# A fused Mamba and attention kernel on one core: convolution taps of half the channels as matrix products, and the first B spread by TensorE

## The chip, the cores and the metric

The kernel runs on one core of a Trainium2 chip. The metric is the device time of one execution in microseconds; smaller is better. In the text, PE is TensorE (PEld its weight loads), DVE is VectorE, ACT is ScalarE, POOL is GpSimd and SP is the engine that issues the transfers. PX, PY, PZ, ring and sums are tensors in PSUM, everything else is in SBUF.

## What is computed

Eight sequences of 256 rows by 256 columns go through a Mamba block and then through a linear attention block, in float32. The core of the first, per batch:

```python
xz = einsum('bsd,ed->bse', xn, in_proj_w)        # xn: normalized, scaled and shifted x
x_in, z = split(xz, 2)                           # 512 channels each
u = silu(causal_conv(x_in, conv_w) + conv_b)     # per channel, 4 taps along the sequence
dt_r, B, C = split(u @ x_proj_w.T, [64, 80])     # B and C: 16 states each
dt = softplus(dt_r @ dt_proj_w.T + dt_proj_b)
h = h * exp(dt * A) + (dt * u) * B               # scan over 256 steps, 512 channels x 16 states
y = sum over states of h * C + u * D_param
x = x + gate * ((y * silu(z)) @ out_proj_w.T)
```

The second block (`q`, `k`, `v`, softmax over q's heads and over k's rows, `k^T v`, `q (k^T v)`, normalization, silu, output product) follows on the same x.

## The kernel before

Channels lie on the 128 partitions, in four blocks (DC = 4); the 256 steps lie along the free axis. The scan of a batch is cut into 16 units: channel block dc, and four of the 16 states (q), so a unit is 128 x 1024. 8 batches make 128 units, numbered g; the text also counts them 0 to 15 in their batch. A unit goes through five steps:

- POOL makes the inputs `dtu * B` into one of ten buffers of `hs` (L530).
- ACT makes the decays `exp(dt * A)`, four instructions into one of the two halves of `ring` (L722).
- DVE scans (L950), and multiplies with C (L957). Of every batch, units 1, 5, 9 and 13 have this product on POOL (L539).
- PE turns and adds the states of the unit into `sums` (L1298, with the skip term L1293 at the start of a channel block).
- After the last unit of a channel block, DVE gates the sum with silu(z) (L964). `gate_y` of block 0 stands behind the products of unit 4 and waits until the sum of unit 3 is made.

Everything else is woven into this by hand. Each engine has a loop over g in which a table of pairs (slot, step) says in which unit a step is issued: step of batch b in g = 16 b + slot. An engine does its entries strictly in the order of the program; ACT can be at most two units ahead of DVE, since `ring` has two halves. Negative slots belong to the batch before: slot -16 is unit 0 of the scans of batch b - 1, so the projections of batch b are made during the first half of these scans. The steps that matter here, in the order in which they depend on each other:

- `in_proj(b, h)` on PE: h = 0 and 1 are the two halves of x_in (two channel blocks each, L1242: four products of 256 columns), h = 2 and 3 are z (L1247). For b >= 2 all four write PX one after the other, so each waits until the one before has been read. Slots -18, -16, -14, -13.
- `conv_last_tap(b, h)` on ACT (L615): the tap without a shift and the bias, from PX into `conv`. Slots -15 and -14.
- `conv_taps(b, h)` on DVE (L916): three shifted taps for two channel blocks, six instructions that read PX and add into `conv`. Slots -16 and -14.
- `copy_z` on ACT (slot -11, L624) empties PX for `in_proj(b, 3)`; the silus of z and of u follow in unit 7, with a table load on either side.
- On PE, `transpose_back` (unit 1), `out_proj` (unit 3, issued before the unit's sum, L1350) and `transpose_y` (unit 3, L1178, waits for ACT's `normalize2` of unit 6) belong to earlier batches.

Batch 0 has a start of its own: x_proj (L1265), the copy of its result `xdbl` (ACT, L654), which SP stores to DRAM and reads back as copies of B and C over all partitions (`broadcast_b`, `broadcast_c`), dt_proj (L1276), softplus, and DVE's own first input (L928), which waits for the first copy of B. `keep_on` is filler work on PE.

## Time and profile before

| | us |
|---|---|
| runs | 569.86, 568.53, 568.95 |
| median | 568.95 |
| profiled execution | 569.01 |
| its span | 567.2 |

| engine | busy, share of the span | instructions |
|---|---|---|
| DVE | 514.6 us, 91% | 566 |
| POOL | 453.0 us, 80% | 318 |
| PE | 437.9 us, 77% | 2456 |
| ACT | 408.6 us, 72% | 897 |

The span is cut by the profile into waits and busy time of each engine. A busy share is an average over the start (34 us), eight batches of scans (some 500 us) and the end (35 us). In a row of the trace in order of time stand the start and the length in us, the engine, the line, the instruction, output and inputs, and how many instructions the row holds; a product of float32 appears as two records, so four products are a row of x8. The ends of PE's records are modelled and overlap the next row's start by some 0.16 us.

### The profile page before, as it was taken

What the parts mean: (1) busy time and instruction counts of PE and PEld (TensorE: products, weight loads), DVE (VectorE), ACT (ScalarE), POOL (GpSimd) and SP (SyncE); (2) the same over time, 40 slices, a digit from 0 to 9 for tenths busy, and PEclk for the clock granted to TensorE, in tenths of its full rate; (3) what the DMA queues carried; (4) which work ended last, traced back from release to release, by engine and by line L of the source; (5) the groups of instructions that cost most, each with busy time, mean ns of one, the idle gap of its engine ahead of it and who ended that gap; (6) DMA issues with size and microseconds to landing.
All of it is one profiled execution on the core that took longest, in us unless ns stands there. A gap on an engine that the chain in (4) does not pass through costs nothing. (4 is left out here: it accounts for less than half of the span.)

```text
span 567.2 us, 7391 instructions
## 1 busy us (share of the span) xinstructions
PE 437.9 (77%) x2456; PEld 361.2 (64%) x2456; DVE 514.6 (91%) x566; ACT 408.6 (72%) x897; POOL 453.0 (80%) x318
## 2 busy tenths in 40 slices
PE   8967666769789787768688678768787777866887
PEld 7646445657676676656576667647674666755776
DVE  2479899999999999999999999999999999999753
ACT  2693677668865998578966999488966988486533
POOL 4049969989998889979998889978997989985121
PEclk8988777896789798998989898998899898779899
DMA  9294032201430044001440045011440045000001
GB/s 269 66 326 125 3 114 85 102 4 54 159 112 0 29 151 154 14 19 40 159 131 1 28 151 165 2 29 43 147 129 1 10 151 166 2 0 20 0 1 37
DMA packets 22366, 45.38 MB, mean 80 GB/s; under 512 B 3685, under 2 KB 13557, under 8 KB 22329
## 3 DMA queue, kind: packets, MB, share of 16 engines
q1 hardware_dynamic: 22328, 44.92, 24.3%
q8 instruction: 19, 0.31, 0.2%
q14 instruction: 19, 0.15, 0.1%
HBM read 42.52 MB, written 2.39 MB: 79 GB/s over the span
## 5 line engine op out<-in xcount | busy, mean ns | idle before, releaser
L530 POOL TENSOR_TENSOR hs<-dtu,Br 128x1024 f32<-128x1024 f32 x127 | 297.0, 2362 | 8.5 <-DMA Br<-bc_rows 8.5
L722 ACT ACTIVATE ring<-dt,Aneg 128x256 f32<-128x256 f32 x512 | 212.9, 465 | 72.6 <-DVE hs L957 68.7
L950 DVE TENSOR_TENSOR_SCAN ring<-ring,hs 128x1024 f32<-128x1024 f32 x97 | 221.4, 2282 | 5.8 <-ACT ring L722 5.4
L1298 PE MATMUL sums<-ident,hs 128*128 128x128 f32 x1024 | 150.7, 303 | 36.3 <-DVE hs L957 36.0
L1298 PEld LDWEIGHTS sums<-ident,hs 128*128 128x128 f32 x1024 | 134.4, 158 | 48.3 <-DVE hs L957 44.7
L957 DVE TENSOR_TENSOR hs<-ring,Cr 128x1024 f32<-128x1024 f32 x97 | 118.8, 1225 | 3.3
L539 POOL TENSOR_TENSOR hs<-hs,Cr 128x1024 f32<-128x1024 f32 x31 | 73.2, 2360 | 42.1 <-DVE hs L950 42.1
L950 DVE TENSOR_TENSOR_SCAN hs<-ring,hs 128x1024 f32<-128x1024 f32 x31 | 70.3, 2269 | 0.0
L1366 PE MATMUL PY<-wqkvo,xT 128*128 128x256 f32 x168 | 46.6, 428 | 0.0
L1293 PE MATMUL sums<-ident,uD 128*128 128x128 f32 x64 | 15.5, 333 | 35.2 <-DVE ygT L964 35.2
L1366 PEld LDWEIGHTS PY<-wqkvo,xT 128*128 128x128 f32 x168 | 37.5, 223 | 6.6
L615 ACT ACTIVATE conv<-PX,par 128x256 f32<-128x256 f32 x28 | 14.3, 560 | 35.8 <-PE PX L1242 35.6
L916 DVE SCALAR_TENSOR_TENSOR conv<-PX,par,conv 128x255 f32<-128x255 f32 (+2 forms) x84 | 33.9, 472 | 6.0 <-ACT conv L615 5.8
L1293 PEld LDWEIGHTS sums<-ident,uD 128*128 128x128 f32 x64 | 9.1, 168 | 38.2 <-DVE hs L957 37.7
L1242 PE MATMUL PX<-xnT,win 128*128 128x256 f32 x112 | 30.6, 421 | 3.6 <-ACT xnT L606 2.5
L1247 PE MATMUL PX<-win,xnT 128*128 128x512 f32 x52 | 27.1, 646 | 4.2 <-DVE conv L916 2.8
L1242 PEld LDWEIGHTS PX<-xnT,win 128*128 128x128 f32 x112 | 22.3, 209 | 8.0 <-ACT xnT L606 3.9
L1350 PE MATMUL PY<-wo,yg 128*128 128x256 f32 x112 | 25.3, 379 | 0.0
L1350 PEld LDWEIGHTS PY<-wo,yg 128*128 128x128 f32 x112 | 21.2, 190 | 5.4 <-issue 2.9
L481 POOL TENSOR_SCALAR ve<-mv 128x2 f32<-128x2 f32 x22 | 4.9, 222 | 24.2 <-DVE mv L899 22.9
L1178 PE MATMUL PZ<-ident,xh 128*128 128x128 f32 x56 | 10.1, 310 | 16.5 <-ACT xh L591 16.5
L1178 PEld LDWEIGHTS PZ<-ident,xh 128*128 128x128 f32 x56 | 7.5, 159 | 21.9 <-ACT xh L591 20.9
(218 smaller groups left out, 694.1 us busy)
## 6 DMA issues: line engine op xcount, KB each, us to landing
Br<-bc_rows SPq DMA_DIRECT2D x32, 512.0 KB, 5.1
Cr<-bc_rows SPq DMA_DIRECT2D x32, 512.0 KB, 4.2
xg<-in_x SPq DMA_DIRECT2D x8, 256.0 KB, 2.9
out<-fin SPq DMA_DIRECT2D x7, 256.0 KB, 4.2
hs<-in_ada_wT SPq DMA_DIRECT2D x3, 512.0 KB, 4.6
win<-in_in_wT SPq DMA_DIRECT2D x2, 512.0 KB, 6.1
hs<-in_W_emb SPq DMA_DIRECT2D x2, 512.0 KB
gate<-gate_rows SPq DMA_DIRECT2D x8, 128.0 KB, 3.1
```

What stands on the lines that cost most here:

```text
L530: nc.gpsimd.tensor_tensor(hs[:, g % DBUF], dtu[:, b % 2, dc, :].unsqueeze(1).to_broadcast([P, NQ, T]), Br[:, NQ * q:NQ * q + NQ, :], ALU.m ...
L539: nc.gpsimd.tensor_tensor(hs[:, g % DBUF], hs[:, g % DBUF], Cr[:, NQ * q:NQ * q + NQ, :], ALU.mult).then_inc(s_hc_pool, 1)
L722: ins = nc.scalar.activation(ring[:, g % 2, j, :], dt[:, b % 2, dc, :], ACT.Exp, scale=Aneg[:, c:c + 1])
L916: V.scalar_tensor_tensor(conv[:, dc, s:], xz_bank(b, h)[:, e, 0:T - s], w, conv[:, dc, s:], ALU.mult, ALU.add).then_inc(s_tap_done, 1)
L950: V.tensor_tensor_scan(driven if by_pool(g) else decays, decays, driven, 0.0, ALU.mult, ALU.add).then_inc(s_scan_done, 1)
L957: V.tensor_tensor(hs[:, g % DBUF], ring[:, g % 2], Cr[:, NQ * q:NQ * q + NQ, :], ALU.mult).then_inc(s_hc_dve, 1)
L1242: ins = M(xz_bank(b, h)[:, e, :], win[:, k, lo:lo + P], xnT[:, k, :], start=(k == 0), stop=(k == KD - 1))
L1247: ins = M(flat(xz_bank(b, h)), xnT[:, k, P * c:P * c + P], win[:, k, DI:2 * DI], start=(k == 0), stop=(k == KD - 1))
L1293: ins = M(YT[:, c, :], uD[:, dc % 2, P * c:P * c + P], ident[:, :], is_transpose=True, start=(c == 0), stop=False, skip_group_check=True)
L1298: ins = M(YT[:, c, :], hs[:, g % DBUF, j, P * c:P * c + P], ident[:, :], is_transpose=True, start=False, stop=(q == UPC - 1 and j == NQ - ...
L1350: ins = M(dst, yg[:, k, P * c:P * c + P], wo[:, k, :], start=(k == 0), stop=(k == DC - 1))
L1366: ins = M(dst, xT_of(b)[:, k, P * c:P * c + P], wqkvo[:, w, k, :], start=False, stop=(k == KD - 1), skip_group_check=True)
```

## The change

There are two parts.

**The taps.** For batches 2 to 7 and h = 1 (`folded`), DVE's six instructions are gone. PE makes the convolution itself: the weights of this half are scaled by each of the four taps, and the four products with xn shifted by 0 to 3 steps are added in PX (`taps_of_block`), per channel block 2 x 4 products instead of 2. The first channel block stands in slot -16, the second in -15. ACT's `conv_last_tap` of that half only adds the bias, and moves from slot -14 to -12. `in_proj(b, 2)` and `in_proj(b, 3)` move one slot back, to -13 and -12, for b >= 2; for batch 1 they stay. The scaled weights are made once by POOL: three of them in the start (`wtap`), from taps that two new transfers of SP spread over the partitions, and the last in unit 14 over the weights themselves.

**The start.** B for unit 0 is spread over the partitions by PE (`first_b`, four products of a column of ones at B's row with `xdbl`, into ring's second half), so DVE's first input reads PSUM instead of waiting for the transfer; the transfer of this part of B goes last but one. DVE copies the first xdbl instead of ACT. ACT does the silu of u's first half ahead of z's, and loads the silu table before it waits. `keep_on` is shorter in two places.

On PE, from the sum of unit 0 to the first row of unit 4 in a batch with folding, before. `sums<-ident,hs` x8 is the sum of a unit (x16 of two), `PX<-xnT,win` the second half of x_in, `PX<-win,xnT` z, `PY<-wo,yg` out_proj, `PZ<-ident,xh` transpose_y:

```order
L1298 MATMUL sums<-ident,hs 128x128 x8
L1242 MATMUL PX<-xnT,win 128x256 x4
L1316 MATMUL PZ<-ident,ygT 128x128 x4
L1316 MATMUL PY<-ident,ygT 128x128 x4
L1298 MATMUL sums<-ident,hs 128x128 x16
L1247 MATMUL PX<-win,xnT 128x512 x2
L1350 MATMUL PY<-wo,yg 128x256 x8
L1298 MATMUL sums<-ident,hs 128x128 x8
L1247 MATMUL PX<-win,xnT 128x512 x2
L1178 MATMUL PZ<-ident,xh 128x128 x4
L1293 MATMUL sums<-ident,uD 128x128 x2
```

The same place after (the first channel block's products are in it, the second's, the same four rows, come behind the transposes and are cut off in the first fence; the second fence goes on from there):

```order
L1382 MATMUL sums<-ident,hs 128x128 x8
L1322 MATMUL PX<-xnT,win 128x256 x2
L1322 MATMUL PX<-xnT,wtap 128x255 x2
L1322 MATMUL PX<-xnT,wtap 128x254 x2
L1322 MATMUL PX<-xnT,wtap 128x253 x2
L1400 MATMUL PZ<-ident,ygT 128x128 x4
L1400 MATMUL PY<-ident,ygT 128x128 x4
L1322 MATMUL PX<-xnT,win 128x256 x2
```

```order
L1382 MATMUL sums<-ident,hs 128x128 x16
L1434 MATMUL PY<-wo,yg 128x256 x8
L1382 MATMUL sums<-ident,hs 128x128 x8
L1306 MATMUL PX<-win,xnT 128x512 x2
L1231 MATMUL PZ<-ident,xh 128x128 x4
L1377 MATMUL sums<-ident,uD 128x128 x2
L1382 MATMUL sums<-ident,hs 128x128 x8
L1306 MATMUL PX<-win,xnT 128x512 x2
```

Sixteen products stand where four stood, ahead of the sums of units 1 to 3; the first half of z is behind the sum of unit 3, and the second half of z behind transpose_y and the sum of unit 4.

On ACT, from the skip term of unit 2 to the copy of z, before (`ring<-dt,Aneg` x4 are the decays of a unit, `conv<-PX,par` is conv_last_tap, `yg` the copies for out_proj, `zs` the copy of z):

```order
L701 ACTIVATE uD<-u,par 128x256
L615 ACTIVATE conv<-PX,par 128x256 x2
L722 ACTIVATE ring<-dt,Aneg 128x256 x4
L731 ACTIVATE yg<-PZ 128x512
L731 ACTIVATE yg<-PY 128x512
L722 ACTIVATE ring<-dt,Aneg 128x256 x8
L624 ACTIVATE zs<-PX 128x512
```

and after:

```order
L746 ACTIVATE uD<-u,par 128x256
L769 ACTIVATE ring<-dt,Aneg 128x256 x4
L778 ACTIVATE yg<-PZ 128x512
L778 ACTIVATE yg<-PY 128x512
L769 ACTIVATE ring<-dt,Aneg 128x256 x4
L658 ACTIVATE conv<-PX,par 128x256 x2
L769 ACTIVATE ring<-dt,Aneg 128x256 x4
L667 ACTIVATE zs<-PX 128x512
```

conv_last_tap of the second half moved behind the decays of unit 4; the copy of z stays behind those of unit 5.

The diff, without the declarations of semaphores:

```diff
--- before.py
+++ after.py
+FOLDED = (1,)
+FOLD_LO, FOLD_N = 2 * P * FOLDED[0], 2 * P * len(FOLDED)
...
+def folded(b, h):
...
+    return b >= 2 and h in FOLDED
...
+def taps_until(b, h):
...
+    return sum(3 * 2 for c in range(b + 1) for k in range(2) if not folded(c, k) and (c, k) <= (b, h))
...
+        wtap = sb("wtap", [P, TAPS - 1, KD, FOLD_N])
...
+        wrow = hs[:, 1, 1:NQ, :]
+        last_row = fin[:, 0, :]
...
-                    broadcast_b(b, 0)
...
+                    broadcast_b(b, 0)
...
+            sp.dma_start(wrow, a["tap_rows"][1:TAPS, FOLD_LO:FOLD_LO + FOLD_N].unsqueeze(0).to_broadcast([P, TAPS - 1, FOLD_N])).then_inc(
+                s_ld_taps, 16)
+            sp.dma_start(last_row, a["tap_rows"][0, FOLD_LO:FOLD_LO + FOLD_N].unsqueeze(0).to_broadcast([P, FOLD_N])).then_inc(
+                s_ld_taps, 16)
...
-                if dc == 0:
+                if dc == 0 or g == UPC:
...
+            def scale_taps():
...
+                pool.wait_ge(s_ld_taps, 32)
+                pool.wait_ge(s_ld_win, 16)
+                for s in range(1, TAPS):
+                    nc.gpsimd.tensor_tensor(wtap[:, s - 1], win[:, :, FOLD_LO:FOLD_LO + FOLD_N],
+                                            wrow[:, s - 1, :].unsqueeze(1).to_broadcast([P, KD, FOLD_N]), ALU.mult).then_inc(s_taps_ready, 1)
+                pool.wait_ge(s_taps_ready, TAPS - 1)
...
+            def scale_last_tap():
...
+                pool.wait_ge(s_xz_mm, 4 + 2)
+                part = win[:, :, FOLD_LO:FOLD_LO + FOLD_N]
+                nc.gpsimd.tensor_tensor(part, part, last_row.unsqueeze(1).to_broadcast([P, KD, FOLD_N]),
+                                        ALU.mult).then_inc(s_taps_ready, 1)
...
+                if g == -6:
+                    scale_taps()
+                if g == 14:
+                    scale_last_tap()
...
+                    tap = 1.0 if folded(b, h) else pcol("conv_w", TAPS * dc + 3, TAPS * dc + 4)
...
-                                         scale=pcol("conv_w", TAPS * dc + 3, TAPS * dc + 4)).then_inc(s_conv0_ready, 1)
+                                         scale=tap).then_inc(s_conv0_ready, 1)
...
             def silu_u(b):
-                act.wait_ge(s_tap_done, 3 * DC * (b + 1))
+                act.wait_ge(s_conv0_ready, DC * (b + 1))
+                act.wait_ge(s_tap_done, taps_until(b, 1))
...
             def copy_xdbl(b):
+                if b == 0:
+                    return
...
-                if b >= 1:
-                    act.wait_ge(s_bc_stored, 16 * b)
+                act.wait_ge(s_bc_stored, 16 * b)
...
+                if g == 1:
+                    act.wait_ge(s_dbu_first, 1)
...
             def silus(b):
...
+                if b == 0:
+                    nc.scalar.preload_act_table_set("silu_and_others")
+                    silu_u_half(0)
...
-                if b == 0:
-                    silu_u_half(0)
-                if b < NB:
...
-                for slot, step in ((-17, normalize0), (-16, modulated), (-15, conv_last_tap_0), (-14, conv_last_tap_1),
+                for slot, step in ((-17, normalize0), (-16, modulated), (-15, conv_last_tap_0), (-12, conv_last_tap_1),
...
-                    late = 2 if step in (conv_last_tap_0, conv_last_tap_1) else 1 if step is modulated else 0
+                    late = 2 if step is conv_last_tap_0 else 1 if step is modulated else 0
...
             def conv_taps(b, h):
...
+                if folded(b, h):
+                    return
...
-                            dve.wait_ge(s_tap_done, 3 * DC * b + 6 * h + 2 * (s - 2) + e + 1)
+                            dve.wait_ge(s_tap_done, taps_until(b, h) - 6 + 2 * (s - 2) + e + 1)
...
+            def first_xdbl():
+                dve.wait_ge(s_xp_mm, 1)
+                V.tensor_copy(xdbl[0:ONES_ROW, :], PX[0:ONES_ROW, 0, :]).then_inc(s_xdbl_ready, 1)
...
-                dve.wait_ge(b_loaded[0], 16)
-                V.tensor_tensor(hs[:, 0], dtu[:, 0, 0, :].unsqueeze(1).to_broadcast([P, NQ, T]), Br[:, 0:NQ, :],
+                dve.wait_ge(s_first_b, 1)
+                V.tensor_tensor(hs[:, 0], dtu[:, 0, 0, :].unsqueeze(1).to_broadcast([P, NQ, T]), ring[:, 1],
...
+                    first_xdbl()
...
+            def wait_x_read(b, h):
...
+                pe.wait_ge(s_conv0_ready, DC * b + 2 * h + 2)
+                if not folded(b, h):
+                    pe.wait_ge(s_tap_done, taps_until(b, h))
...
-                        pe.wait_ge(s_tap_done, 3 * DC * b + 6 * (h - 1))
+                        wait_x_read(b, h - 2)
...
-                    pe.wait_ge(s_tap_done, 3 * DC * b + 6 * h)
+                    wait_x_read(b, h - 1)
...
-                    keep_on(12)
+                    keep_on(4)
...
+            def taps_of_block(b, h, e):
...
+                if e == 0:
+                    wait_x_read(b, h - 1)
+                    if b == 2:
+                        pe.wait_ge(s_taps_ready, TAPS)
+                lo = P * (2 * h + e)
+                for s in range(TAPS):
+                    for k in range(KD):
+                        w = wtap[:, s - 1, k, lo - FOLD_LO:lo - FOLD_LO + P] if s else win[:, k, lo:lo + P]
+                        ins = M(PX[:, e, s:T], w, xnT[:, k, 0:T - s], start=(s == 0 and k == 0),
+                                stop=(s == TAPS - 1 and k == KD - 1), skip_group_check=True)
+                if e == 1:
+                    ins.then_inc(s_xz_mm, 1)
...
+            def first_b():
...
+                pe.wait_ge(s_ld_ident, 16)
+                for n in range(NQ):
+                    row = ident[0:ONES_ROW + 1, RANK + n:RANK + n + 1]
+                    ins = M(ring[:, 1, n, :], row.to_broadcast([ONES_ROW + 1, P]), xdbl[:, :], start=True, stop=True)
+                ins.then_inc(s_first_b, 1)
...
+                if (b, h) == (0, 0):
+                    first_b()
...
-                    keep_on(8)
+                    keep_on(4)
...
             def in_proj_1(b):
-                in_proj(b, 1)
+                if folded(b, 1):
+                    taps_of_block(b, 1, 0)
+                else:
+                    in_proj(b, 1)
...
+            def in_proj_1b(b):
+                if folded(b, 1):
+                    taps_of_block(b, 1, 1)
...
-                for slot, step in ((17, transpose_back), (-19, transpose_x), (-18, in_proj_0), (-16, in_proj_1), (-14, in_proj_2),
-                                   (-13, in_proj_3), (39, output), (-9, x_proj), (-8, dt_proj_0), (-6, dt_proj_1),
+                for slot, step in ((17, transpose_back), (-19, transpose_x), (-18, in_proj_0), (-16, in_proj_1),
+                                   (-15, in_proj_1b), (-13, in_proj_2), (-12, in_proj_3), (39, output), (-9, x_proj), (-8, dt_proj_0), (-6, dt_proj_1),
...
-                    b = due_by(g, slot, -2 if step is in_proj_1 else 2 if step in (in_proj_2, in_proj_3) else 0)
+                    b = due_by(g, slot, -2 if step is in_proj_1 else 1 if step in (in_proj_2, in_proj_3) else 0)
...
+        "tap_rows": np.asarray(L0_cond_conv_w).reshape(DI, TAPS).T[::-1],
...
```

## Rows read from the trace of the kernel before

**Rows 1.** The page: engines' busy time, and two of its groups of instructions.
```profile
PE 437.9 (77%) x2456; PEld 361.2 (64%) x2456; DVE 514.6 (91%) x566; ACT 408.6 (72%) x897; POOL 453.0 (80%) x318
...
L539 POOL TENSOR_TENSOR hs<-hs,Cr 128x1024 f32<-128x1024 f32 x31 | 73.2, 2360 | 42.1 <-DVE hs L950 42.1
...
L916 DVE SCALAR_TENSOR_TENSOR conv<-PX,par,conv 128x255 f32<-128x255 f32 (+2 forms) x84 | 33.9, 472 | 6.0 <-ACT conv L615 5.8
```

**Rows 2.** DVE in order of time, 287 to 323 us: start us, us, engine, line, instruction.
```profile
298.88 1.22 DVE L957 TENSOR_TENSOR hs<-ring,Cr 128x1024 f32<-128x1024 f32 x1
300.25 2.43 DVE L916 SCALAR_TENSOR_TENSOR conv<-PX,par,conv 128x255 f32<-128x255 f32 x6
302.59 0.74 DVE L896 BATCH_NORM_STATS2 st<-qe 128x6 f32<-128x256 f32 x2
...
303.54 2.27 DVE L950 TENSOR_TENSOR_SCAN ring<-ring,hs 128x1024 f32<-128x1024 f32 x1
...
310.44 0.41 DVE L964 TENSOR_TENSOR ygT<-sums,zs 128x256 f32<-128x256 f32 x1
...
313.55 2.29 DVE L950 TENSOR_TENSOR_SCAN ring<-ring,hs 128x1024 f32<-128x1024 f32 x1
...
322.50 2.30 DVE L950 TENSOR_TENSOR_SCAN ring<-ring,hs 128x1024 f32<-128x1024 f32 x1
```

**Rows 3.** PE in order of time, same stretch; in brackets the idle time before.
```profile
293.81 2.08 PE L1428 MATMUL PY<-att,qT 128*128 128x128 f32 x8 [1.13 <-DVE att L1002]
...
297.26 1.89 PE L1242 MATMUL PX<-xnT,win 128*128 128x256 f32 x8
298.99 0.60 PE L1316 MATMUL PZ<-ident,ygT 128*128 128x128 f32 x4
...
302.73 1.98 PE L1247 MATMUL PX<-win,xnT 128*128 128x512 f32 x4 [0.61 <-DVE conv L916]
304.55 3.62 PE L1350 MATMUL PY<-wo,yg 128*128 128x256 f32 x16
308.01 1.04 PE L1298 MATMUL sums<-ident,hs 128*128 128x128 f32 x8
309.34 1.98 PE L1247 MATMUL PX<-win,xnT 128*128 128x512 f32 x4 [0.29 <-ACT zs L624]
313.70 1.11 PE L1178 MATMUL PZ<-ident,xh 128*128 128x128 f32 x4 [2.38 <-ACT xh L591]
...
315.02 1.91 PE L1298 MATMUL sums<-ident,hs 128*128 128x128 f32 x8
```

**Rows 4.** ACT in order of time, same stretch.
```profile
299.19 1.02 ACT L615 ACTIVATE conv<-PX,par 128x256 f32<-128x256 f32 x2 [6.48 <-PE PX L1242]
...
308.71 0.57 ACT L624 ACTIVATE zs<-PX 128x512 f32<-128x512 f32 x1
310.56 1.67 ACT L722 ACTIVATE ring<-dt,Aneg 128x256 f32<-128x256 f32 x4 [1.28 <-DVE hs L957]
...
317.05 0.58 ACT L636 ACTIVATE zs<-PX 128x512 f32<-128x512 f32 x1
...
320.80 2.47 ACT L722 ACTIVATE ring<-dt,Aneg 128x256 f32<-128x256 f32 x6
```

**Rows 5.** Busy time of PE, PEld, DVE, ACT, POOL; granted clock, DMA share, GB/s.
```profile
314.00:318.00 4.00, 3.78 (x22) 3.38 (x21) 3.93 (x7) 3.97 (x8) 4.00 (x3) 0.61 0.01 5
```

**Rows 6.** DVE in order of time, 96 to 133 us: the gating of unit 4, batch 1.
```profile
120.11 0.41 DVE L964 TENSOR_TENSOR ygT<-sums,zs 128x256 f32<-128x256 f32 x1
```

**Rows 7.** DVE, then ACT and POOL, in order of time, in the start.
```profile
32.62 1.23 DVE L928 TENSOR_TENSOR hs<-dtu,Br 128x1024 f32<-128x1024 f32 x1 [1.96 <-DMA Br<-bc_rows]
...
26.47 0.38 ACT L654 ACTIVATE xdbl<-PX 96x256 f32<-96x256 f32 x1
...
30.70 1.67 ACT L722 ACTIVATE ring<-dt,Aneg 128x256 f32<-128x256 f32 x4
...
26.56 0.23 POOL L487 TENSOR_SCALAR nb<-nb 128x2 f32<-128x2 f32 x1
```

3 lines of the change are left out of this document (added).

## Prediction

> **What bounds the kernel now.** I read the page first, then which engine waits for which, then DVE, PE and ACT in order of time through one batch, and last the start. DVE is busy 91% of the span [rows 1]. In the scan part it has next to no idle time, so whatever makes DVE wait there sets the time. The stretch from 287 to 323 us holds units 0 to 8 of batch 4 of the scans, and the projections of batch 5 are made in it. It repeats alike in scan batches 2 to 6. Who is close behind DVE in it:
>
> - DVE's taps of the second half stand at 300.25, behind the products of unit 2; the next entry starts 2.34 us later, at 302.59 [rows 2].
> - PE starts the attention product at 293.81, released by DVE, and works almost without a gap until 311: the idle times printed are 0.61 and 0.29 us [rows 3]. Of what DVE needs, it is little ahead: the sum of unit 3 takes from 308.01 to 309.05 [rows 3], and DVE's gating L964, which needs it, starts at 310.44 [rows 2].
> - ACT waits 6.48 us before the second half's convolution, and once more 1.28 before 310.56 [rows 4]. From 310.56 it has no gap: decays of unit 6, skip term, normalize, decays of unit 7, two table loads around the silus, then the decays of unit 8 from 320.80. Four decays take 1.67 [rows 4], so these end at 322.47, and DVE's scan of unit 8 starts at 322.50 [rows 2].
>
> So the 91% hides two other engines, with 1.4 and 0 us of slack, at two points just behind the edit.
>
> **The change, part by part.**
>
> *DVE's taps go.* Six batches lose six instructions each (all of them in before: 96, of 472 ns [rows 1]). By starts a group costs 302.59 - 300.25 = 2.34 us [rows 2], 14.0 in six. If nothing else moved, that is the gain.
>
> *PE's products come, in units 0 and 1.* The old block of four starts at 297.26 and its follower at 298.99: 1.73 us, 0.43 each [rows 3]. Now there are 16, 12 more: 12 x 0.43 = 5.2 us, where PE has no gap. in_proj_2 goes from before out_proj to behind the sum of unit 3: that takes 304.55 - 302.73 = 1.82 out ahead of the sum, and the 0.61 of idle time, a wait for the removed taps [rows 3]. The sum of unit 3 starts at 308.01 + 5.2 - 1.82 - 0.61 = 310.8. It takes 0.9 (1.04 less the 0.16 by which neighbouring rows overlap), so it ends at 311.7.
>
> *DVE meanwhile.* The products of unit 2 end at 298.88 + 1.22 = 300.1; stats2 takes 0.95 (302.59 to 303.54), scan and products of units 3 and 4 some 3.45 each (from 303.54 to 310.44 both) [rows 2]. So DVE reaches the gating at 308.0. ACT keeps up: its wait in unit 2 is gone, and its copies of yg follow transposes that end 1.7 us later. DVE waits from 308.0 to 311.7, and the gating comes 1.3 us *later* than before, the saved 2.34 notwithstanding.
>
> *ACT behind it.* in_proj_2 follows at 311.7 and takes 1.98 [rows 3]: 313.6. ACT's copy of z (0.57) needs it and stands ahead of the decays of unit 6. Before, it was done at 309.28, in idle time [rows 4]. Now these decays start at 314.1 instead of 310.56, 3.5 us later. Having no gap from there, ACT carries these 3.5 to scan 8 whole.
>
> *PE again.* transpose_y, formerly behind in_proj_3, is now ahead of it, and waits for normalize2, which stands behind those decays. Before, it started 313.70 - 310.56 = 3.14 after them [rows 3, 4]; now at 317.2. The transposes and the sum of unit 4 took 3.2, from 313.70 to 316.93 [rows 3]; over 314 to 318 the granted clock was 0.61, mostly the lower of its two levels (1.2 of 2.4 GHz), after PE had stood idle 2.38 us [rows 3, 5]. This time it stands idle from 313.6 to 317.2, so I take the same 3.2: in_proj_3 starts at 320.4, ends at 322.4. ACT wants it for the second silu of z, 317.05 - 310.56 = 6.49 after its decays [rows 4], at 320.6, and waits 1.8. From there to the decays of unit 8 it is 3.75 (317.05 to 320.80), so these start at 326.1 instead of 320.80: **+5.3 us**. With the transposes and the sum at the upper level (1.6) it would be +3.8. I take 5.0, nearer to the slow value since the idle time ahead grows. DVE scans unit 6 at 314.1 + 1.67 = 315.8, reaches unit 8 the old 8.95 later, at 324.7, and waits 3.1 for the decays. Behind unit 8 the distances are the old ones and DVE bounds again, so nothing is given back. Scan batches 2 to 6: 5 x 5.0 = 25.0.
>
> *Scan batch 1* has neither attention nor transpose_y yet, so PE has more room. Its cost lies between 0 and 5.3; its gating of unit 4 stood at 120.11 [rows 6]. The copy of z is late there too, in_proj_3 is not; I take 1.9. Scan batches 0 and 7 have no folded half.
>
> *The start.* Before, DVE's first input waits 1.96 us for the transfer of B, starts at 32.62 and takes 1.23, and the first scan follows at 33.9 [rows 7]. With B from PE this wait goes; next are the decays, from 30.70, which end at 32.37 [rows 7]. u ahead of z brings x_proj forward by up to the 0.6 of one silu. But ACT's normalization, which follows, is held by POOL's nb, done at 26.79, and ACT already started it behind xdbl (26.47 to 26.85) [rows 7]; so this part gives 0.1 to 0.3. The first scan starts at some 32.1: -1.8. What hides the rest: the four products for B (0.43 each, or double at the lower level) lie beside ACT's softplus; on SP the other copies of B and C move one place forward, and B 0, now last, is next wanted for unit 4; POOL's three scalings fall where it has nothing to do yet, each half the size of one of 2360 ns [rows 1], the fourth where it is ahead, and its waits for DVE's scans, 42.1 us in all [rows 1], are the cover. SP's two new transfers (0.5 MB) go out before its long wait for xdbl. Bounds: 0, if the wait for in_proj_2 in unit 5 takes it back, and -3, if all of the 1.96 and the time of u arrive.
>
> **Sum.** The profiled execution took 569.0 (span 567.2 and 1.8 around it), the median of the runs is 568.95, the same. 569.0 + 25.0 + 1.9 - 1.8 = **594.1 us**, 4.4% slower. Own range: 3.8 to 5.8 in five batches, 0 to 5.3 in batch 1, 0 to -3 at the start, not all at one end: 583 to 604.
>
> **A rule weighed.** PE is busy 77% on average and DVE 91% [rows 1], which makes moving work from DVE to PE look free. In the rows of the stretch PE has no gap. The Trainium skill (Perfetto Trace Analysis, Identifying Performance Opportunities) says to optimize the engine with the highest occupancy first, and that PE's busy share is no good measure of its headroom. By the first half of this the time would be the first rival's; by the rows it is the forecast's.
>
> **Rivals.**
>
> 1. *PE has the room, and DVE's saving arrives* (faster): 569.0 - 14.0 - 1.8 = 553 us. It needs PE's products to cost next to nothing beside the old ones: 313.6 for in_proj_2 less 5.2 is 308.4, and DVE is at the gating at 308.0. The point from which it decides: in_proj_2 done by 310.0, that is 12 products in 1.6 us, 0.13 each. For it speaks PE's average; against it 0.43 us by starts for this shape, already at the upper level [rows 3].
> 2. *PE's clock pays for half.* If its higher load holds the upper level, the attention product and the sum behind it are 1.4 us shorter, the transposes and sum 4 1.6 shorter. Then scan 8 is some 2.3 later than before: 569.0 + 5 x 2.3 + 1 - 1.8 = 580. Against it: the lower level follows PE's waits of 1.13 and 2.38 us [rows 3, 5], and these stay or grow. The Trainium skill (TensorE: Matmul & The Clock Gate, Part 1) says that activity releases the throttle, which would speak for it.
> 3. *More is late.* The lower level also catches in_proj_3 (1.98 becomes some 3.7): +7 a batch, 604 and more.
> 4. *It cancels out*: 569. I see no mechanism.
>
> **Chances.** Forecast (583 to 604) 0.72; second rival (567 to 583, most of it above 574) 0.12; third 0.05; first, or a part of it, 0.09; fourth 0.02. The range 574 to 604 holds 0.82. A measurement of this kernel tells about 0.2% from no change. Faster by more than that 0.09, within it 0.02, slower 0.89.
>
> **What would show it.** Right: in scan batches 2 to 6 DVE idle for 3 to 4 us before the gating of unit 4, released by PE's sum, and some 3 us before the scan of unit 8, released by ACT; ACT waiting for PE before the copy of z and before the second silu of z; these batches each some 5 us longer from first scan to first scan, batch 1 some 2; the first scan at 32.1. Wrong: each batch 2 us shorter, with these waits under a microsecond (first rival); or a granted clock near 1 behind the transposes (second); or the decays of unit 8 not behind in_proj_3.

## The result, and the profile after

The changed kernel takes 592.23 us (median of 4, 591.25 to 593.18); the kernel before, in the same session, 569.40 (median of 4, 568.53 to 571.23). The ratio is 1.040, 95% interval 1.037 to 1.042: **slower by 4%**. The profiled execution took 592.05. The forecast was 594, slower.

Its page, engines' busy time, against [rows 1]:

```profile
span 590.3 us, 7643 instructions
...
PE 470.4 (80%) x2592; PEld 390.6 (66%) x2592; DVE 503.2 (85%) x531; ACT 407.2 (69%) x896; POOL 457.7 (78%) x322
```

DVE lost 35 instructions and 11.4 us of work, PE gained 32.5, and the span grew by 23.1. DVE's idle time is where it went. In the view of who waits for whom stand the engine and line, the releaser, the us in total, the times and the longest; before, the first of these two waits was 5.4 us in 6 times, and the second stood only once for 1.2, in the end:

```profile
DVE ring L1002 <- ACT ring L769: 23.7, 15, 4.2
DVE ygT L1016 <- PE sums L1382: 20.0, 8, 3.6
```

By batch, from the start of the scan of one unit 0 to the next (for batch 7, to the scan of its last unit):

| scan batch | 0 | 1 | 2 | 3 | 4 | 5 | 6 | 7 |
|---|---|---|---|---|---|---|---|---|
| before, us | 65.1 | 60.7 | 63.7 | 63.5 | 63.3 | 63.5 | 63.1 | 55.4 |
| after, us | 65.0 | 61.4 | 66.7 | 68.3 | 68.3 | 68.3 | 68.3 | 56.1 |

Batch 4 begins at 293.90, 6.88 later than before (287.02); subtract 6.88 to set the next rows beside [rows 2 to 4]. DVE in order of time (start us, us, engine, line, instruction, in brackets the idle time before it and who ended it):

```profile
313.60 1.22 DVE L1009 TENSOR_TENSOR hs<-ring,Cr 128x1024 f32<-128x1024 f32 x1
318.43 0.42 DVE L1016 TENSOR_TENSOR ygT<-sums,zs 128x256 f32<-128x256 f32 x1 [3.60 <-PE sums L1382]
...
322.33 2.30 DVE L1002 TENSOR_TENSOR_SCAN ring<-ring,hs 128x1024 f32<-128x1024 f32 x1 [0.70 <-ACT ring L769]
...
334.42 2.30 DVE L1002 TENSOR_TENSOR_SCAN ring<-ring,hs 128x1024 f32<-128x1024 f32 x1 [3.21 <-ACT ring L769]
```

PE in the same stretch:

```profile
300.69 2.08 PE L1512 MATMUL PY<-att,qT 128*128 128x128 f32 x8 [0.73 <-DVE att L1054]
...
304.41 1.03 PE L1322 MATMUL PX<-xnT,win 128*128 128x256 f32 x4
305.27 2.73 PE L1322 MATMUL PX<-xnT,wtap 128*128 128x255 f32 x12
307.84 0.60 PE L1400 MATMUL PZ<-ident,ygT 128*128 128x128 f32 x4
...
317.36 1.04 PE L1382 MATMUL sums<-ident,hs 128*128 128x128 f32 x8
318.23 1.88 PE L1306 MATMUL PX<-win,xnT 128*128 128x512 f32 x4
323.77 0.66 PE L1231 MATMUL PZ<-ident,xh 128*128 128x128 f32 x4 [3.66 <-ACT xh L633]
...
324.48 1.81 PE L1382 MATMUL sums<-ident,hs 128*128 128x128 f32 x8
326.08 2.83 PE L1306 MATMUL PX<-win,xnT 128*128 128x512 f32 x4
```

And ACT:

```profile
320.15 0.60 ACT L667 ACTIVATE zs<-PX 128x512 f32<-128x512 f32 x1 [5.40 <-PE PX L1306]
320.64 1.66 ACT L769 ACTIVATE ring<-dt,Aneg 128x256 f32<-128x256 f32 x4
...
328.95 0.60 ACT L679 ACTIVATE zs<-PX 128x512 f32<-128x512 f32 x1 [1.73 <-PE PX L1306]
...
332.72 3.26 ACT L769 ACTIVATE ring<-dt,Aneg 128x256 f32<-128x256 f32 x8
```

Read it as one chain. The 8 products of one column block (16 entries of the trace) take 307.84 - 304.41 = 3.43 us, and there are two blocks: 6.9 us where the old four products took 1.73 [rows 3]. So the sum of unit 3 ends at some 318.2, and DVE stands 3.60 us before the gating. in_proj_2 is next; only when it is done can ACT copy z, and the decays of unit 6 stand behind that copy. Then PE idles 3.66 for ACT's normalization and makes in_proj_3 late, so ACT idles 1.73 for it. The decays of unit 8 start at 332.72, in the old count 325.84 against 320.80: 5.04 us late. DVE waits 3.21 for them. The new waits (3.60, 0.70 and 3.21) less the 2.34 of taps that are gone make 5.2, against 5.04 of longer period.

### The profile page after: what moved, and what is told of

Same layout as the page of the kernel before. It is cut to its first block and busy times, and to the rows that moved or that the text cites. A ratio compares the mean times of both kernels' runs of the same rounds, so it can differ in the third digit from the quotient of the medians.

```text
span 590.3 us, 7643 instructions
## 1 busy us (share of the span) xinstructions
PE 470.4 (80%) x2592; PEld 390.6 (66%) x2592; DVE 503.2 (85%) x531; ACT 407.2 (69%) x896; POOL 457.7 (78%) x322
## 5 line engine op out<-in xcount | busy, mean ns | idle before, releaser
L1382 PE MATMUL sums<-ident,hs 128*128 128x128 f32 x1024 | 148.7, 302 | 17.4 <-DVE hs L1009 17.4
L1450 PE MATMUL PY<-wqkvo,xT 128*128 128x256 f32 x168 | 48.5, 441 | 0.0
L1450 PEld LDWEIGHTS PY<-wqkvo,xT 128*128 128x128 f32 x168 | 39.3, 234 | 7.3
L1322 PE MATMUL PX<-xnT,wtap 128*128 128x255 f32 (+2 forms) x144 | 32.8, 377 | 0.0
L667 ACT ACTIVATE zs<-PX 128x512 f32<-128x512 f32 x7 | 4.2, 597 | 40.0 <-PE PX L1306 40.0
L1016 DVE TENSOR_TENSOR ygT<-sums,zs 128x256 f32<-128x256 f32 x32 | 13.3, 416 | 20.0 <-PE sums L1382 20.0
L1322 PEld LDWEIGHTS PX<-xnT,wtap 128*128 128x128 f32 x144 | 27.4, 190 | 3.5
L1306 PE MATMUL PX<-win,xnT 128*128 128x512 f32 x52 | 29.3, 695 | 0.0
L1231 PEld LDWEIGHTS PZ<-ident,xh 128*128 128x128 f32 x56 | 6.1, 141 | 34.2 <-ACT xh L633 33.9
L964 DVE SCALAR_TENSOR_TENSOR conv<-PX,par,conv 128x255 f32<-128x255 f32 (+2 forms) x48 | 19.4, 472 | 5.7 <-ACT conv L658 5.7
L1434 PEld LDWEIGHTS PY<-wo,yg 128*128 128x128 f32 x112 | 20.7, 190 | 2.5
```

The source lines that it names most:

```text
L964: V.scalar_tensor_tensor(conv[:, dc, s:], xz_bank(b, h)[:, e, 0:T - s], w, conv[:, dc, s:], ALU.mult, ALU.add).then_inc(s_tap_done, 1)
L1306: ins = M(flat(xz_bank(b, h)), xnT[:, k, P * c:P * c + P], win[:, k, DI:2 * DI], start=(k == 0), stop=(k == KD - 1))
L1322: ins = M(PX[:, e, s:T], w, xnT[:, k, 0:T - s], start=(s == 0 and k == 0), stop=(s == TAPS - 1 and k == KD - 1), skip_group_check=True)
L1382: ins = M(YT[:, c, :], hs[:, g % DBUF, j, P * c:P * c + P], ident[:, :], is_transpose=True, start=False, stop=(q == UPC - 1 and j == NQ - ...
L1434: ins = M(dst, yg[:, k, P * c:P * c + P], wo[:, k, :], start=(k == 0), stop=(k == DC - 1))
L1450: ins = M(dst, xT_of(b)[:, k, P * c:P * c + P], wqkvo[:, w, k, :], start=False, stop=(k == KD - 1), skip_group_check=True)
```

## Experiments

Twelve kernels ran. In the table each stands with its own runs of the kernel before.

| run | us, median (n) | before | ratio, 95% interval |
|---|---|---|---|
| e1 start alone | 567.56 (12) | 569.78 | 0.997 (0.996 to 0.999) |
| e2 taps alone | 593.02 (4) | 569.78 | 1.041 (1.039 to 1.044) |
| e3 no shifted products | 571.54 (10) | 569.78 | 1.003 (1.000 to 1.005) |
| e4 before, PE delayed | 594.28 (4) | 569.78 | 1.043 (1.041 to 1.046) |
| e5 in_proj_3 early | 574.53 (5) | 569.61 | 1.008 (1.005 to 1.011) |
| e6 e3 and e5 together | 558.53 (4) | 569.61 | 0.979 (0.975 to 0.983) |
| e7 start alone, bias late | 569.77 (12) | 569.61 | 1.001 (0.998 to 1.003) |
| e8 folded, reordered | 558.98 (5) | 569.61 | 0.981 (0.978 to 0.984) |
| e9 e8, sum 4 first | 556.34 (6) | 569.31 | 0.978 (0.974 to 0.982) |
| e10 e9, bias on GpSimd | 555.16 (6) | 569.31 | 0.975 (0.972 to 0.979) |
| e11 e8 without folding | 571.59 (10) | 569.31 | 1.005 (1.003 to 1.008) |
| e12 e10, scaling later | 554.46 (6) | 569.32 | 0.974 (0.970 to 0.977) |

### The two halves of the change apart: e1 and e2

e1 is the changed kernel with no folded half and without what serves it alone:

```
 def folded(b, h):
-    return b >= 2 and h in FOLDED
+    return False
...
-                if g == -6:
-                    scale_taps()
-                if g == 14:
-                    scale_last_tap()
```

> The start of the change alone (first input from TensorE's copy of B, u ahead of z, fewer filler products); all taps are VectorE's again, and the tap rows and GpSimd's four scaling operations are gone. Theory T (the start gives what it gave in the changed kernel, first scan 1.5 us earlier; and the 2.4 us which VectorE lost at unit 8 of batch 0 came from GpSimd's shifted phase behind the last scaling, so it does not come back here): 565.5 to 568, ratio 0.993 to 0.998, the 128x8 operation of unit 8 in batch 0 again near 0.23 us. Rival S (the time of unit 8 moves with the start itself): first scan 1.5 earlier, unit 8 late again, 568.5 to 569.5.

e2 keeps the folding and undoes the start: SP's old order of copies, ACT's copy of xdbl, the input from `Br`, z ahead of u, the old fillers.

```
-                    act.wait_ge(s_dbu_first, 1)
...
-                dve.wait_ge(s_first_b, 1)
+                dve.wait_ge(b_loaded[0], 16)
...
-                    first_xdbl()
```

> The taps of the change alone; the start is as before. Theory T (12 more products per batch ahead of the sums of units 1 to 3, in_proj_2 behind the sum of unit 3, in_proj_3 behind the transposes of the second normalisation): +4.6 to +5.2 per batch in batches 3 to 6, +3 in batch 2, +1 to +2 in batch 1, +0.8 in batch 7, in all 592 to 595, ratio 1.039 to 1.046. Rival S (a part of the loss comes from the start's changed phase): under 590.

Both times are as theory T had them; of its parts one missed, batch 1 of e2 grew by 0.75 and not by 1 to 2. The start is worth -2.2 us (0.8 to 2.5 by the interval), the taps +23.2, together 21.0; the whole was 22.8, which their intervals don't tell apart. The periods of e2 are those of the changed kernel within 0.05 us in batches 1 to 6. One reason in e1's expectation was wrong: the small operation at unit 8 of batch 0 took 1.48 us, not 0.23. It has a section of its own below.

### What PE's time ahead of the sum costs: e4

```
                     c = h - 2
-                    for k in range(KD):
-                        ins = M(flat(xz_bank(b, h)), xnT[:, k, P * c:P * c + P], win[:, k, DI:2 * DI], start=(k == 0),
-                                stop=(k == KD - 1))
+                    for _ in range(4 if b >= 2 and h == 2 else 1):
+                        for k in range(KD):
+                            ins = M(flat(xz_bank(b, h)), xnT[:, k, P * c:P * c + P], win[:, k, DI:2 * DI], start=(k == 0),
+                                    stop=(k == KD - 1))
```

> The kernel before, VectorE's taps kept, with in_proj_2 of batches 2 to 7 made four times into the same bank (the same result), 6 more products, 5 to 6 us more of TensorE ahead of the sum of unit 3; nothing is taken from any engine. Theory T (TensorE's work ahead of the sum of unit 3 comes out in the gating product's wait): the gating wait in batches 3 to 6 is 2.5 to 5 us, periods +2.5 to +5, in all 583 to 595. Rival R (TensorE at 77% busy has room for 5 us in the stretch): periods +0.5 at most, 569 to 572.

Nothing was taken from DVE or ACT, and the time is that of the changed kernel. PE and DVE of e4 in batch 4:

```profile
314.08 7.13 PE L1248 MATMUL PX<-win,xnT 128*128 128x512 f32 x16 [0.37 <-DVE conv L916]
```
```profile
325.58 0.42 DVE L964 TENSOR_TENSOR ygT<-sums,zs 128x256 f32<-128x256 f32 x1 [3.71 <-PE sums L1299]
```

The equal time is no evidence by itself, since it is made up differently: 4.7 us in batch 1, where the gating waits 4.63, and 3.4 to 4.5 in each of batches 2 to 6. The wait is the evidence. The 6 products more (12 entries) made in_proj_2 7.13 us long instead of 1.98 [rows 3], 5.15 more, and of this 3.71 came out as DVE's wait at the gating; the other 1.4 was the slack of the sum of unit 3 that the prediction had read off (309.05 against 310.44 [rows 2, 3]). With PE at 79% busy there was no room for 5 us in this place. (Unit 8 has no wait in e4 in batches 2 to 5, so e4 shows the first of the changed kernel's two large waits and not the second.) Rival R, the first rival of the prediction in another coat, is out.

### The products, or their order: e3, e5, e6

e3 leaves the 12 shifted products of each folded half out and keeps the order of all engines:

```
-                for s in range(TAPS):
+                for s in range(1):
```

> The changed kernel without the 12 products of the shifted taps of each folded half, from batch 2 on: the shifted taps of channels 256 to 511 are left out of what is computed, their unshifted tap stays (TensorE makes 4 products there, as before), VectorE makes none of them, the order of all engines is that of the changed kernel. Theory T (the length of the products is the cost): the gating product of unit 3 no longer waits for TensorE for over 0.5 us, the period of batches 3 to 6 is 62.0 to 63.8 us, in all 561 to 570. Rival O (the new order of TensorE, with in_proj_2 behind the sum of unit 3 and in_proj_3 behind the transposes, is the cost, whatever the length): periods over 65, in all over 578.

Both theories missed. The gating's wait went to nothing, as T said; but 571.5 is above T's range, and the periods of batches 2 to 4 are 64.2 to 64.6 (63.1 and 63.3 in 5 and 6). DVE has 2.34 us less work in each batch, waits 2.3 to 3.9 at unit 8, where the kernel before waited 0.08, and so gives all of it back. ACT, PE and DVE of e3, batch 4:

```profile
318.73 0.60 ACT L679 ACTIVATE zs<-PX 128x512 f32<-128x512 f32 x1 [2.98 <-PE PX L1306]
```
```profile
312.30 1.11 PE L1231 MATMUL PZ<-ident,xh 128*128 128x128 f32 x4 [3.66 <-ACT xh L633]
...
315.34 3.36 PE L1306 MATMUL PX<-win,xnT 128*128 128x512 f32 x4
```
```profile
324.20 2.30 DVE L1002 TENSOR_TENSOR_SCAN ring<-ring,hs 128x1024 f32<-128x1024 f32 x1 [3.88 <-ACT ring L769]
```

So the place of in_proj_3, behind transposes that wait for ACT, has a price of its own without the long products. Part of it is PE's clock: the granted clock was 0.50 over 312 to 316, and in_proj_3 took 3.36 us where [rows 3] has 1.98. e5 moves it alone, one slot forward, in the complete changed kernel; e6 does so in e3, so it too leaves the shifted taps out:

```
-                                   (-15, in_proj_1b), (-13, in_proj_2), (-12, in_proj_3), (39, output), (-9, x_proj), (-8, dt_proj_0), (-6, dt_proj_1),
+                                   (-15, in_proj_1b), (-13, in_proj_2), (-13, in_proj_3), (39, output), (-9, x_proj), (-8, dt_proj_0), (-6, dt_proj_1),
...
-                    b = due_by(g, slot, -2 if step is in_proj_1 else 1 if step in (in_proj_2, in_proj_3) else 0)
+                    b = due_by(g, slot, -2 if step is in_proj_1 else 1 if step is in_proj_2 else 2 if step is in_proj_3 else 0)
```

> The changed kernel with in_proj_3 straight behind in_proj_2, ahead of the transposes of the second normalisation instead of behind them and the sum of unit 4. Theory T2 (the loss has two parts: the products' length, which comes out at the gating product, and in_proj_3's place, which comes out at scan 8 through the second silu): the wait of that silu (1.73 us) goes, scan 8 waits 1.4 to 1.7 us instead of 3.21, periods of batches 3 to 6 about 66.6, in all 582 to 585. Rival (the place of in_proj_3 is free, since ScalarE's chain is bound elsewhere): within 2 us of 592.

> The changed kernel without the 12 products of the shifted taps of each folded half (they are left out of what is computed; the unshifted tap stays) and with in_proj_3 straight behind in_proj_2: the run without the products, and without the one piece of order that is under suspicion. Theory T2: the run that only left the products out lost at scan 8 what VectorE saved, 3.2 to 3.9 us of wait, of which the silu's wait for TensorE was 2.98; here that wait is gone, scan 8 waits under 1 us, periods 61.0 to 61.8, in all 556 to 561. Rival (something else of the order holds ScalarE): periods stay over 63, 568 or more.

The silu's wait of 1.73 is gone in e5, scan 8 waits 1.36 (expected 1.4 to 1.7). But the time fell by 17.7 us, not by 8: the periods are 64.83 in all of batches 2 to 6, 1.9 less in batch 2 and 3.5 less in the others. Most of the rest is this row of PE, which stands ahead of anything that was moved, and the gating behind it:

```profile
294.12 1.16 PE L1512 MATMUL PY<-att,qT 128*128 128x128 f32 x8 [1.14 <-DVE att L1054]
```
```profile
310.23 0.42 DVE L1016 TENSOR_TENSOR ygT<-sums,zs 128x256 f32<-128x256 f32 x1 [1.96 <-PE sums L1382]
```

The attention product took 1.16 us instead of 2.08, the sum behind it 1.04 instead of 1.59, and the gating waited 1.96 instead of 3.60. That is PE's clock, at its upper level here (granted clock 1.00 over 293 to 297), which is taken up below. So the 17.7 us are 5 x 1.85 at unit 8 (3.21 less 1.36), the order; 4 x 1.64 at the gating of batches 3 to 6, the clock; and some 2 in the start and in batches 1 and 7. e6 gives 558.5, within its range of 556 to 561, with periods of 61.4 and a wait of 0.79 at scan 8. The four corners:

| | 12 products made | left out |
|---|---|---|
| in_proj_3 behind the transposes | 592.2 | 571.5 |
| in_proj_3 straight behind in_proj_2 | 574.5 | 558.5 |

Leaving the products out gives 20.7 in the one order and 16.0 in the other; moving in_proj_3 gives 17.7 and 13.0. The first is the length, the second the order together with the clock. The order without the clock is some 9 of the 17.7, as just added up. The prediction's sum had both in it, the length and the 1.8 us of in_proj_3's place.

### A kernel that keeps the products and is faster: e8 and e11

e8 leaves nothing out. Its moves: out_proj from ahead of the sum of unit 3 to behind it (3.46 us out of the gating's way); in_proj_3 ahead of the sum of unit 4 instead of behind it, still behind the transposes of the second normalization, but with ACT's normalization for them already in unit 4, where ACT idled for 1.23 and 5.40 us; the first z turned into its silu straight from PSUM, without the copy; and the second z's silu last of the silus.

```
-                b = due(g, 19)
-                if b is not None:
-                    out_proj(b)
                 if 0 <= g < NB * U and not by_pool(g):
...
-                for slot, step in ((17, transpose_back), (-19, transpose_x), (-18, in_proj_0), (-16, in_proj_1),
-                                   (-15, in_proj_1b), (-13, in_proj_2), (-12, in_proj_3), (39, output), (-9, x_proj), (-8, dt_proj_0), (-6, dt_proj_1),
+                for slot, step in ((17, transpose_back), (19, out_proj), (-19, transpose_x), (-18, in_proj_0), (-16, in_proj_1),
+                                   (-15, in_proj_1b), (-13, in_proj_2), (35, transpose_y), (-13, in_proj_3), (39, output), (-9, x_proj), (-8, dt_proj_0), (-6, dt_proj_1),
...
-                for slot, step in ((-17, normalize0), (-16, modulated), (-15, conv_last_tap_0), (-12, conv_last_tap_1),
+                for slot, step in ((-17, normalize0), (-16, modulated), (-15, conv_last_tap_0), (36, normalize2), (-12, conv_last_tap_1),
...
             def copy_z(b):
-                if b == 0:
+                if b != 1:
                     return
...
+                elif b >= 2:
+                    act.wait_ge(s_xz_mm, 4 * b + 3)
+                    act.wait_ge(s_ygT_ready, DC * (b - 1))
+                    nc.scalar.activation(zs[:, b % 2, 0, :], flat(xz_bank(b, 2)), ACT.Silu).then_inc(s_z_ready, 2)
...
+                if 1 <= b < NB:
+                    silu_z_second(b)
```

> The changed kernel with five moves, nothing left out: TensorE's out_proj behind the sum of unit 3 instead of ahead of it; then in_proj_2, the transposes of the second normalisation, in_proj_3, then the sum of unit 4; ScalarE's second normalisation in unit 4, ahead of the copy of the folded half, where ScalarE idles; no copy of the first z but its silu straight from PSUM; u's silu and the transposed y's ahead of the second z's. Theory T2: the gating product no longer waits 3.6 us (under 0.9), ScalarE's chain from decays 6 to decays 8 shortens from 12.1 to about 9.6 us, scan 8 waits under 1 us, periods 61.0 to 62.3, in all 556 to 562: TensorE's 12 products fit in once what else stands ahead of the sum is moved. Rival (TensorE has no room for them at any order, it then delays the gating product of unit 7, or the dt chain of the next batch): periods 64 or more, 570 or more.

e11 has the same moves and no folding.

> The five moves of the folded and reordered kernel without the folding: VectorE makes all taps, TensorE 4 products for the second half, the start is the changed one. Theory T2 (the moves only make room for TensorE's products; without them VectorE sets the time): 566 to 570, ratio 0.994 to 1.002, periods of batches 2 to 6 of 63 to 64 us. Rival (the moves are worth something by themselves, and the folding nothing): 562 or less.

e8 is 558.98, 33 us below the changed kernel and 1.9% below the one before. DVE, ACT and PE of e8 in batch 4:

```profile
303.05 0.41 DVE L1020 TENSOR_TENSOR ygT<-sums,zs 128x256 f32<-128x256 f32 x1
...
315.85 2.30 DVE L1006 TENSOR_TENSOR_SCAN ring<-ring,hs 128x1024 f32<-128x1024 f32 x1 [0.72 <-ACT ring L771]
```
```profile
308.77 0.60 ACT L674 ACTIVATE zs<-PX 128x512 f32<-128x512 f32 x1
...
312.23 0.60 ACT L681 ACTIVATE zs<-PX 128x512 f32<-128x512 f32 x1 [1.00 <-PE PX L1310]
```
```profile
309.42 2.77 PE L1310 MATMUL PX<-win,xnT 128*128 128x512 f32 x4 [2.22 <-ACT zs L674]
```

The gating has no wait, scan 8 has 0.72, the periods of batches 3 to 6 are 61.4 (62.9 in batch 2). The moves were made together; what each is worth no run shows. e11 came out at 571.6, 1.6 above its range. DVE in batch 3 of e11, and the out_proj that it waits for:

```profile
249.41 0.69 DVE L1020 TENSOR_TENSOR x<-PY,gate 128x512 f32<-128x512 f32 x1 [1.50 <-PE PY L1430]
```
```profile
243.74 5.64 PE L1430 MATMUL PY<-wo,yg 128*128 128x256 f32 x16
```

out_proj stands late, and at the lower clock (5.64 us instead of 3.62) it is too late for `gate_x`, which waits for it in four batches, 4.4 us in all. So the moves cost some 4 us over e1, and are worth nothing by themselves. In the new order folding is worth 571.6 - 559.0 = 12.6 us, but 4 of these are e11's own loss. Against e1, the better of the two kernels without folding, e8 gains 8.6 us, and the changed kernel loses 24.7 (592.2 less 567.6). The same twelve products.

### The idle time ahead of in_proj_3: e9

```
-                                   (-15, in_proj_1b), (-13, in_proj_2), (35, transpose_y), (-13, in_proj_3), (39, output), (-9, x_proj), (-8, dt_proj_0), (-6, dt_proj_1),
+                                   (-15, in_proj_1b), (-13, in_proj_2), (35, transpose_y), (-12, in_proj_3), (39, output), (-9, x_proj), (-8, dt_proj_0), (-6, dt_proj_1),
...
-                    b = due_by(g, slot, -2 if step is in_proj_1 else 1 if step is in_proj_2 else 2 if step is in_proj_3 else 0)
+                    b = due_by(g, slot, -2 if step is in_proj_1 else 1 if step in (in_proj_2, in_proj_3) else 0)
```

> The folded and reordered kernel with one move: in_proj_3 behind the sum of unit 4 instead of ahead of it, so that TensorE does not stand idle for 2.2 us ahead of in_proj_3. In the folded and reordered run in_proj_3 took 2.8 us at the lower clock, the second z's silu waited 1.0 us for it, and scan 8 0.72. Theory K (the lower clock behind TensorE's idle time is what that wait is made of): in_proj_3 takes 1.9 us, the silu waits under 0.3 us, scan 8 under 0.1, 0.6 to 0.7 less in each of batches 3 to 6, in all 555.5 to 556.5. Rival (the clock stays low, since TensorE still idles for about a microsecond there): 558.5 to 559.5.

In batches 2, 3 and 5 the theory holds: in_proj_3 takes 1.98 (2.77 in e8, behind 2.2 us of idle time; here PE is idle 1.1), in batch 5 the silu waits 0.22, DVE has no wait, and the period is 60.6, nearly all of it DVE's work. Batch 6 is as long, with a wait of 0.88 at unit 8. The time is 556.34 (553.5 to 559.3), as expected within its spread. Batch 4 is 62.9 long: DVE waits 1.04 for decays, 0.26 at the gating and 0.83 for out_proj. PE in it, and in batch 5:

```profile
285.16 2.08 PE L1516 MATMUL PY<-att,qT 128*128 128x128 f32 x8 [1.13 <-DVE att L1058]
```
```profile
348.10 1.16 PE L1516 MATMUL PY<-att,qT 128*128 128x128 f32 x8 [1.13 <-DVE att L1058]
```

### The small operations beside GpSimd: e7, e10, e12

At unit 8 of batch 0, DVE makes four 128x8 operations. Before, they took 0.23 us each, beside an idle GpSimd. DVE and POOL of the changed kernel:

```profile
72.26 0.41 DVE L1120 TENSOR_SCALAR m1s<-mods,par 128x8 f32<-128x8 f32 x1
72.59 2.40 DVE L1120 TENSOR_SCALAR m1b<-mods,par 128x8 f32<-128x8 f32 x1
74.90 0.22 DVE L1120 TENSOR_SCALAR m1s<-mods,par 128x8 f32<-128x8 f32 x1
```
```profile
71.38 1.27 POOL L591 TENSOR_TENSOR win<-win,fin 128x512 f32<-128x512 f32 x1
72.60 2.36 POOL L552 TENSOR_TENSOR hs<-dtu,Br 128x1024 f32<-128x1024 f32 x1
```

The first ends at 72.67, 0.02 behind POOL's scaling; the second at 74.99, 0.03 behind POOL's product; the third is at its 0.22 again, beside an idle POOL. e7 moves them, in e1:

```
-            for at, step in ((3, setup_gate8), (8, add_emb_bias)):
+            for at, step in ((3, setup_gate8), (11, add_emb_bias)):
```

> The start of the change alone, with VectorE's small operations on the embedding's biases (four of 128x8 and their neighbours) moved from behind unit 8 to behind unit 11 of batch 0. Theory G (a 128x8 operation of VectorE that begins while GpSimd's 128x1024 operation runs ends only with it; it cost 1.25 us in the start alone, 2.2 in the changed kernel): unit 8 takes 4.85 us instead of 6.10, and the operations behind unit 11, where GpSimd is among its small ones, cost up to 0.8 more than 0.2 each, so 0.5 to 1.3 us below the start alone, 566.2 to 567.1, ratio 0.994 to 0.9965. Rival (the length of the 128x8 operation has another cause, such as its PSUM operand or the table): unit 11 takes the same 1.2 more instead, 567.5.

Both forecasts of the time missed: 569.8. The place was badly chosen: POOL was at work there again, and three operations were caught instead of one. DVE and POOL of e7:

```profile
82.45 0.67 DVE L1112 TENSOR_SCALAR m1s<-mods,par 128x8 f32<-128x8 f32 x1
...
83.16 1.30 DVE L1112 TENSOR_SCALAR m1s<-mods,par 128x8 f32<-128x8 f32 x1
...
84.62 2.41 DVE L1116 TENSOR_TENSOR m1b<-m1b,mods 128x8 f32<-128x8 f32 x2
```
```profile
81.81 1.28 POOL L519 TENSOR_TENSOR dt<-dt,conv 128x512 f32<-128x512 f32 x1
83.17 1.27 POOL L522 TENSOR_TENSOR dtu<-dt,u 128x512 f32<-128x512 f32 x1
...
84.58 4.65 POOL L548 TENSOR_TENSOR hs<-dtu,Br 128x1024 f32<-128x1024 f32 x2
```

The first two end within 0.03 us of the POOL operation beside them (83.09 and 84.44 by start and length), and the first of the two additions in the last row (86.95 by itself) 0.02 behind the first of POOL's two products (86.93). So theory G's mechanism is shown, three times in one place. Unit 11 took 8.18 us instead of 3.45; the operations alone are 1.0 of it, by unit 8, which takes 4.84 with them in the kernel before and 3.80 without them in e7. e10 gives the six operations to GpSimd, in e9 (the same operations are taken out of DVE's program, which the cut leaves out):

```
+            def emb_rows():
+                pool.wait_ge(s_emb_ready, 1)
+                for k in range(KD):
+                    for dst, w in ((m1s, "ln2_w"), (m1b, "ln2_b")):
+                        nc.gpsimd.tensor_scalar(dst[:, k, :], mods[:, 2 * KD + k, :], 1.0, pcol(w, k, k + 1), ALU.add,
+                                                ALU.mult).then_inc(s_emb_ready, 1)
...
+                if g - BEHIND == 9:
+                    emb_rows()
```

> The kernel of the run before in this list (folded, reordered, in_proj_3 behind the sum of unit 4), with the four 128x8 operations on the embedding's biases and the two additions behind them given to GpSimd, ahead of its product of unit 9 of batch 0, where it idles for 2.9 us. Theory G (those operations of VectorE end only when GpSimd's running operation does): unit 8 of batch 0 takes 3.8 to 4.0 us instead of 7.1, of which 2.2 was the stall and 1.0 the operations' own time, 2.5 to 3.3 us less in all than the run before. Rival (GpSimd becomes late for unit 9 or for the inputs behind it): under 1 us less.

Unit 8 takes 3.91 us instead of 7.07: the local forecast is met. The time fell by 1.2, not by 2.5 to 3.3, inside the spread of the runs. In the profiled one DVE gave it back at the next gating:

```profile
99.95 0.42 DVE L1032 TENSOR_TENSOR ygT<-sums,zs 128x256 f32<-128x256 f32 x1 [3.32 <-PE sums L1390]
```
```profile
94.42 1.97 PE L1390 MATMUL sums<-ident,hs 128*128 128x128 f32 x8 [2.56 <-POOL hs L561]
```

POOL's product of unit 13, which these sums need, was late. e12 takes 1.3 us out of POOL's way there:

```
-                if g == 14:
+                if g == 20:
                     scale_last_tap()
```

> The kernel of the run with the bias operations on GpSimd, with GpSimd's scaling of the last tap (1.3 us) moved from ahead of its inputs of unit 14 to ahead of those of batch 1's unit 4, nothing else. Theory P (there VectorE gained 3.2 us at unit 8 of batch 0 and waited 3.3 us for the sum at the first gating product of batch 1, because GpSimd's product of unit 13 came too late for TensorE, which then had three sums and in_proj_0 still to do): GpSimd's product of unit 13 ends 1.2 to 1.4 us earlier, the gating product waits 1.8 to 2.4 us, 0.8 to 1.5 us less in all than the run before. Rival (TensorE's in_proj_0, waiting for ScalarE, sets that wait): the wait stays over 3 us and the time within 0.5 us.

The gating's wait fell from 3.32 to 0.16, more than theory P said, and PE's wait for POOL from 2.56 to 0.17. Yet batch 2 begins at 154.9 us in both: 1.15 us was lost at unit 1 of batch 0, and 1.72 ahead of unit 7 of batch 1, where DVE waits for POOL's addition of the residual. At 554.5 the median is 0.7 lower, which these spreads (552.8 to 556.2 and 552.9 to 557.7) don't tell from nothing. With DVE's waits gone, POOL, 83% busy, is what is late next in batches 0 and 1. e12 has the lowest median of the study, 2.65% below the kernel before.

## Why the prediction was right, point by point

- **DVE's taps**, 14 us in six batches: right. DVE's busy time fell by 11.4, since the copy of xdbl (0.4) and the time that the operations beside POOL took in unit 8 (2.4) came in. How much of it can arrive: e8 is 8.6 us below e1, and e9 11.2.
- **12 products at 0.43 us**: right. Eight products took 3.43, sixteen 6.86, against 1.73 of before: 5.1 more. The sum of unit 3 was forecast for 310.8 and started at 317.36 - 6.88 = 310.48. The step as a cause stands by e4: 5.15 us on PE in this place gave 3.71 of wait.
- **DVE's wait at the gating**, 308.0 to 311.7: 3.60 measured, 3.7 forecast. In part this was luck. The prediction says that the stretch "repeats alike in scan batches 2 to 6", and took the attention product's 2.08 us for all of them. In the trace of before that is so in batch 4 (and 1.87 in batch 2), but in batches 3, 5 and 6 it took 1.16, at the upper level:

```profile
357.08 1.16 PE L1428 MATMUL PY<-att,qT 128*128 128x128 f32 x8 [1.13 <-DVE att L1002]
```

There the wait would have been near the 1.96 of the changed kernel's batch 2. That four batches of five ran at the lower level after the change follows from no step of the prediction; with the levels of before in batches 3, 5 and 6, the estimate from these waits is some 5 us less (3 x 1.64).
- **The late copy of z and the decays of unit 6** at 314.1: measured 313.76.
- **PE again**: right in its end, by two errors that cancelled. The transposes and the sum of unit 4 were to take 3.2 at the lower clock level and took 2.3: the transposes were at the upper level (0.66 against 1.11 in [rows 3]), the sum of unit 4 mostly at the lower (1.81 against 1.04 in e5); the granted clock was 1.00 over 320 to 324 and 0.57 over 324 to 328. The lower level also caught in_proj_3, which took 2.83 instead of 1.98 (the third rival, in part). The silu's wait was 1.73, forecast 1.8.
- **+5.3, taken as 5.0**: 4.8 to 5.2 in batches 3 to 6, 3.0 in batch 2. There the attention product ran at the upper level (1.16 us) and the gating waited 1.96: the half of the second rival that speaks of that product came true for one batch, and in e5 for all. 5 x 5.0 = 25.0 was 22.8.
- **Batch 1**, +1.9: it was +0.7. The gating waited 1.63 and scan 6 0.70, and the removed taps gave most of it back.
- **The start**, -1.8: the first scan came 1.5 earlier (32.45). In the profiled executions of all runs it lies between 31.6 and 33.3 with the new start, and between 33.9 and 35.0 with the old. Its other effect, 2.4 us at unit 8 of batch 0 for DVE operations beside POOL, was in no step. DVE's wait of 2.54 in unit 5 fell to 0.86, which was not in it either, and the two hid each other: batch 0 has its old length.
- Batch 7 and the tail, at nothing: +0.8 and +0.4.
- **The range**: the bounds of the parts add up to 585 and 603; the 583 and 604 of the forecast are wider by rounding outwards.

Forecast minus result in the profiled execution: 594.1 - 592.05 = 2.0, of which 2.2 are batches 2 to 6, 1.2 batch 1, and -1.4 the rest.

So the mechanism was right, and the closeness of the number has some luck in it. What the prediction did not ask is what the order alone costs. It priced length and order (the "+1.8" of in_proj_3 among them), but its rivals all turned on the length or the clock. No rival said that the products fit if other things made room.

## What to carry to other kernels

Before work is moved to an engine with a low busy share, find the next result of that engine which the bound engine needs, and count what stands ahead of it in the queue; the slack at that one point (here 1.4 us) is the room, not the share. Then see which of the things ahead of it need not be there: out_proj (3.5 us) was wanted by nobody until unit 5, and with it behind the sum, and the other moves of e8, the same change came out 8.6 us below e1 instead of 24.7 above it. A thing moved back has a next reader too: in e11 out_proj came up to 1.5 us late for it. When an engine's queue has an instruction that waits for a second engine, what stands behind it is late for the third; put the independent work first.
